# The second turn of the node stage of layers 0 and 1: from TensorE to VectorE squares and a move inside SBUF

## The reference, cut to what matters

```python
x = _layernorm(x + relu(concat(x, max_diff) @ W + b))        # layer 0
# layer 1
x = swish(x @ lin_W.T + lin_b)
h1 = swish((agg1 @ rel1.T + b + x @ root1.T) @ lin1.T + b)   # agg: sums over edges, 0 for most nodes
h2 = swish((agg2 @ rel2.T + b + x @ root2.T) @ lin2.T + b)
h = concat(h1, h2) @ cat_W.T + cat_b + x
for i in range(3):
    h = swish(h @ lins_W[i].T + lins_b[i]) + h
```

## Time and profile before

| | us |
|---|---|
| three executions | 5523.48, 5533.62, 5541.32 |
| median | 5533.62 |
| profiled execution: span from the first to the last instruction | 5523.1 |

### The profile page before, as it was taken

One profiled execution on the slowest core, in us unless ns is written; L12 is line 12 of the kernel. 1 busy time (PEld: TensorE's weight loads), 2 busy tenths in 40 slices (PEclk: granted clock), 3 DMA queues, 4 the chain that ended last, 5 costly groups with the idle time before them and its releaser, 6 DMA issues. The chain is left out here.

```text
span 5523.1 us, 86293 instructions
## 1 busy us (share of the span) xinstructions
PE 4551.3 (82%) x20518; PEld 2819.0 (51%) x20518; DVE 4178.7 (76%) x8262; ACT 3700.6 (67%) x9029; POOL 4058.2 (73%) x4123
## 2 busy tenths in 40 slices
PE   7999999999999999999999999999677756661000
PEld 4566666666666644444444477777455534451000
DVE  5766666666666658888888899999788854457776
ACT  4777777777777754444444488888688864446665
POOL 6777777777777768777777477777777767777777
PEclk9999999999999999999999999999855555665555
DMA  4556656556565646555555599999799867775443
GB/s 121 142 140 135 136 139 139 139 139 140 139 140 135 140 112 195 178 179 179 176 180 176 170 356 367 365 367 365 270 291 287 276 208 228 230 236 163 134 137 103
DMA packets 558505, 1084.50 MB, mean 196 GB/s; under 512 B 131183, under 2 KB 225065, under 8 KB 558279
## 3 DMA queue, kind: packets, MB, share of 16 engines
q1 hardware_dynamic: 452918, 931.29, 54.7%
q0 software_dynamic: 100352, 149.23, 11.2%
q10 hardware_dynamic: 5008, 1.60, 0.1%
HBM read 648.47 MB, written 438.76 MB: 197 GB/s over the span
## 5 line engine op out<-in xcount | busy, mean ns | idle before, releaser
L832 ACT ACTIVATE p_s<-p_ps,cols 128x512 f32<-128x512 f32 x588 | 404.5, 688 | 317.3 <-PE p_ps L774 207.7
L685 POOL DMA_INDIRECT p_xs<-in_x,src_cols x388 | 376.4, 970 | 221.1 <-DVE p_r L900 131.5
L1163 POOL DMA_INDIRECT ring_rows<-t_rows,home_cols x384 | 446.8, 1164 | 120.4 <-issue 88.6
L692 POOL DMA_INDIRECT home<-edge_row_cols,scatter_cols x392 | 414.8, 1058 | 131.2 <-issue 119.2
L182 POOL DMA_INDIRECT out<-u_res,scatter_cols x392 | 407.2, 1039 | 121.8 <-issue 117.8
L175 POOL DMA_INDIRECT u_rows<-t_rows,home_cols x392 | 388.6, 991 | 145.6 <-issue 118.5
L175 POOL DMA_INDIRECT ring_rows<-t_rows,home_cols x400 | 396.7, 992 | 128.2 <-issue 115.2
L685 POOL DMA_INDIRECT p_xd<-in_x,dst_cols x388 | 391.4, 1009 | 107.5 <-issue 89.0
L1172 POOL DMA_INDIRECT home_cols<-home,src_cols x376 | 379.8, 1010 | 111.4 <-issue 85.9
L1259 ACT ACTIVATE q_s<-q_ps,cols 128x512 f32<-128x512 f32 x294 | 202.1, 687 | 355.9 <-PE q_ps L1236 310.7
L900 DVE TENSOR_TENSOR p_r<-p_s,p_r 128x512 f32<-128x512 f32 x392 | 267.9, 683 | 194.0 <-ACT p_s L832 192.5
(11 more groups left out here) (310 smaller groups left out, 14446.8 us busy)
## 6 DMA issues: line engine op xcount, KB each, us to landing
p_x<-in_x SPq DMA_DIRECT2D x98, 512.0 KB, 6.5
t_rows<-p_o SPq DMA_DIRECT2D x98, 512.0 KB
hT<-ring_own SPq DMA_DIRECT2D x98, 512.0 KB
q_hn<-hT SPq DMA_DIRECT2D x98, 512.0 KB
r_h<-hT SPq DMA_DIRECT2D x98, 512.0 KB
r_x<-t_rows SPq DMA_DIRECT2D x98, 512.0 KB
t_rows<-r_y SPq DMA_DIRECT2D x98, 512.0 KB
t_rows<-r_x SPq DMA_DIRECT2D x98, 512.0 KB
```

Of the source, the lines that this page charges most:

```text
L685: nc.gpsimd.indirect_dma_start(out=rows[:, j, :], out_offset=None, in_=a["x"], in_offset=bass.IndirectOffsetOnAxis(ap=idx[:, j:j + 1], axi ...
L692: nc.gpsimd.indirect_dma_start(out=tab["home"], out_offset=bass.IndirectOffsetOnAxis(ap=s["scat"][:, k:k + 1], axis=0), in_=s["at"][:, k:k ...
L832: nc.scalar.activation(act_out[i][:, :], flat(bank_r), ACT.Silu, bias=col(LS0 + i)).then_inc(r_act[i], 1)
L1163: nc.gpsimd.indirect_dma_start(out=rows[:, e % 4, j, :], out_offset=None, in_=tab["t1"], in_offset=bass.IndirectOffsetOnAxis(ap=s["home"][ ...
```

## The change

The normalised rows `o` are no longer turned by TensorE. VectorE turns them in 32x32 squares into `o_turned` (`turn_squares`), at the head of a step, one step after ScalarE scaled them. When both blocks of a pair are turned, SyncE issues 16 transfers (`swap_groups`), each from 32 partitions of `o_turned` to 32 partitions of `x1T`, 256 numbers of 4 bytes in each partition, which bring every square to its place. The product by `lin` reads `x1T` in the order that `by_column` gives, and waits for these transfers.

The product by `lin` and the swish behind it move from lag 3 to lag 6, `R1` to `cat` from lag 4 to 7, the three rounds of `lins` from 5 to 8, the store of `hT` by one round. POOL's hold moves with them (`2 * e - 8`). The turn of `o` on TensorE, ScalarE's copy of it and the waits for both are gone. The pipeline has 206 steps (`NB + 10`), before 202, of which the last with work for TensorE is 203, before 200.

```diff
+def swap_groups(sp, across, turned, sem):
+    for a in range(4):
+        for c in range(4):
+            sp.dma_start(across[32 * c:32 * (c + 1), a], turned[32 * a:32 * (a + 1), c]).then_inc(sem, DMA)
+
+def by_column(across):
+    return across.rearrange("p a (j i) -> p j a i", j=G)
...
-        xT, x1T, xx = sb("p_xT", [P, 2, BLK]), sb("p_x1T", [P, 2, BLK]), sb("p_xx", [P, 4, BLK])
+        xT, xx = sb("p_xT", [P, 2, BLK]), sb("p_xx", [P, 4, BLK])
+        o_turned, x1T = sb("p_oT", [P, 2, 4, 2, P]), sb("p_x1T", [P, 2, 4, 2, P])
...
-        STEPS = 2 * QB + 4
+        STEPS = NB + 10
...  (SyncE)
-                n = t - 10
+                n = t - 12
                 if live(n, NB):
                     sp.wait_ge(r_added[2], n + 2)
                     sp.dma_start(tab["hT"][n // 2]...
+                n = t - 6
+                if live(n, NB):
+                    q = n // 2
+                    sp.wait_ge(o_squared, n + 2)
+                    after(sp, lined, n - 2)
+                    swap_groups(sp, x1T[:, q % 2], o_turned[:, q % 2], x1_in[q % 2])
...  (POOL)
-                    after(pool, r_added[0], 2 * e - 5)
+                    after(pool, r_added[0], 2 * e - 8)
...  (TensorE; lags 4 and 5 become 7 and 8)
-                n = t.back(3)
-                if n.live(NB):
-                    pe.wait_ge(applied, n.b + 1)
-                    ...
-                    transpose4(nc, bank_t, o[:, n.of(4)], s["ident"]).then_inc(x1_turned, 1)
...
-                n = t.back(3)
+                n = t.back(6)
                 if n.live(NB):
-                    pe.wait_ge(x1_copied, n.b + 1)
+                    q = n.pair()
+                    pe.wait_ge(x1_in[q.of(2)], landed(2, q, 16))
                     after(pe, h1_ready, n.b)
-                    nc.tensor.matmul(flat(bank_l), s["lin"][:, :], x1T[:, n.of(2), :],
+                    nc.tensor.matmul(flat(bank_l), s["lin"][:, :], by_column(x1T[:, q.of(2), :, n.slot % 2]),
                                      start=True, stop=True).then_inc(lined, 1)
...  (ScalarE)
-                n = t.back(3)
-                if n.live(NB):
-                    act.wait_ge(x1_turned, n.b + 1)
-                    after(act, lined, n.b - 1)
-                    nc.scalar.activation(x1T[:, n.of(2), :], flat(bank_t), ACT.Copy).then_inc(x1_copied, 1)
...  (VectorE, between residual(2) of lag 9 and residual(0) of lag 8)
+                n = t.back(3)
+                if n.live(NB):
+                    q = n.pair()
+                    dve.wait_ge(applied, n.b + 1)
+                    if n.past(4):
+                        dve.wait_ge(x1_in[q.of(2)], landed(2, q.back(2), 16))
+                    turn_squares(nc, o_turned[:, q.of(2), :, n.slot % 2].rearrange("p c (j i) -> p c j i", j=G),
+                                 o[:, n.of(4)]).then_inc(o_squared, 1)
```

More of the change, by code:

```diff
@@ L583, in nodes01 @@
         squares_saved, e_squared = [sem(f"squares_saved{i}") for i in range(2)], sem("e_squared")
-        (x_turned, x_copied, x1_turned, x1_copied, product, biased, summed, counted, guarded, rooted, scaled,
+        o_squared, x1_in = sem("o_squared"), [sem(f"x1_in{i}") for i in range(2)]
+        (x_turned, x_copied, product, biased, summed, counted, guarded, rooted, scaled,
          applied, lined, active, u_done1, u_done2, h1_ready, h2_ready, cat_done, r0_ready) = (sem(m) for m in (
-             "x_turned", "x_copied", "x1_turned", "x1_copied", "product", "biased", "summed", "counted",
+             "x_turned", "x_copied", "product", "biased", "summed", "counted",
              "guarded", "rooted", "scaled", "applied", "lined", "active", "u_done1", "u_done2", "h1_ready", "h2_ready",
@@ L737, in bank_t_left @@
                     pe.wait_ge(xd_copied, e.b + 1)
-                elif t.back(4).live(NB):
-                    pe.wait_ge(x1_copied, t.back(4).b + 1)
                 elif t.back(1).live(NB):
@@ L749, in step @@
                     transpose4(nc, bank_t, x[:, t.of(4)], s["ident"]).then_inc(x_turned, 1)
-                n = t.back(5)
+                n = t.back(8)
                 if n.live(NB):
@@ L755, in step @@
                                      start=True, stop=True).then_inc(r_done[0], 1)
-                n = t.back(4)
+                n = t.back(7)
                 if n.live(NB):
@@ L806, in step @@
                     pe.wait_ge(xd_in[e.of(2)], landed(2, e, G))
-                    if t.back(3).live(NB):
-                        pe.wait_ge(x1_copied, t.back(3).b + 1)
-                    elif t.live(NB):
-                        pe.wait_ge(x_copied, t.b + 1)
-                    else:
-                        bank_t_left(t)
+                    after(pe, x_copied, t.b + 1, NB)
                     transpose4(nc, bank_t, xd[:, e.of(2)], s["ident"]).then_inc(xd_turned, 1)
-                n = t.back(5)
+                n = t.back(8)
                 if n.live(NB):
```

12 lines of the change are left out of this document (4 added, 8 removed).

## The result

The changed kernel takes 5500.6 us in the median of six runs (5490.3 to 5509.0), the kernel before 5529.5 in six, the three of the table above among them (5520.9 to 5541.3). The ratio is 0.9949, with a 95% interval of 0.9936 to 0.9963: 29 us faster (20 to 35 by the interval), where 41 had been forecast. The profiled span is 5496.3 us against 5523.1, the mean granted clock 0.859 against 0.862.

A forecast was written before the change was run, and what follows sets the result against it. TensorE was taken to bound nodes01. Steady pairs -66, fill and drain +18, SyncE's pile-ups +7 gave -41 us, so 5533.6 became 5492.6 us; the range meant to hold 8 times in 10 was 5466 to 5524.

The forecast's parts named there:

- The bound and the steady pair: Steady steps of nodes01: TensorE sets the pace, VectorE's chain some even steps; a pair falls 0.70 to 19.24, 66 us off.
- The new turn hidden, strides free: VectorE's turn of the normed rows: 0.71 us, hidden in idle time; the product by lin reads squares at no cost.
- The transfers: SyncE's sixteen moves a round: stores 3.0, issues 7.6, landing 3.1, so 13.7 us after the scan; 5.4 to spare.
- the bound from the other side: Pessimistic figure for the moves: 0.68 us an issue, 10.9 in all, landing 6.5, together 20.4 us, too late.
- L: Time from the scan's end in an even step to the last landing of that round's moves; forecast 13.7 us.
- the third rival: Moves come late in every round, L823 waits for them; decides from 19.1 us after the scan; 5559 us, chance 0.10.
- The rules of the ports: Skill pages: 32-partition moves at half rate, some 2.4 us a round; a VectorE-GpSimd port lock could cost POOL 1.4 a pair.
- POOL as bound: Rival in nodes01: slower POOL transfers make the pair some 19.55 us; 5522 us, chance 0.13.
- TensorE as the bound throughout: Rival in nodes01: VectorE's chain gives way by 0.2 us, even step 9.08, pair 19.08; 5475 us, chance 0.17.
- Fill and drain, and the pile-ups: Start and end of nodes01: three more steps cost 18 us (14 to 22), SyncE's two pile-ups 7 (2 to 15).
- The stages behind `nodes01` are the same instructions.: Stages after nodes01: unchanged, so the sum gave them no term and the difference was put on the whole time.
- The end on the slower side: Chance of a slower kernel, over 5550 us: 0.09, with moves late in every round as the mechanism.

## Why the prediction came out as it did

**Sign and range right, and the changed stage gave 37.5 to 41.1 us of the 41 summed. The medians moved by 29, and where the other 12 went is only shown in part.** By the prediction's own steps:

- *The bound and the steady pair.* Right. TensorE lost its 0.43, and every second even step became VectorE's. Forecast were 9.09 and 9.29 for the two kinds of even step; measured 9.08 and 9.26, with 0.24 of wait. The sum put 0.05 for starting again into the even step and 10.00 for the odd one. Measured, the start costs 0.06 to 0.10 and stands in the odd step, which takes 10.06 to 10.08 from L772 to L772. The pair comes out at 19.24 as summed, instead of 19.94, so 0.70 x 95 = 66 us. That the even step is set by this chain is shown by moving 0.7 us out of it.
- *The new turn hidden, strides free.* Right: 0.70 us each. The passes of L829 stay at 0.59.
- *The transfers.* The conclusion was right, its number wrong. The term "16 issues 7.6 us" was taken from the nearest row in shape, L149, which reads DRAM (still 7.61 here). A move inside SBUF costs 0.68 to issue, the bound from the other side. The last issue ends 14.2 us after the scan, and the landing fits into the remaining 4.4. So in this round L lies between 14.2 and 18.6, not at 13.7, and under the 19.1 from which the third rival decides. The margin is smaller than the forecast said. The third rival had the right issue time and the wrong landing: it added 6.5 from a row that lies behind a queue of half-megabyte transfers.
- *The rules of the ports.* By the Trainium skill (SBUF — State Buffer, "Door 1: The DMA port swizzle") a move of 32 neighbouring partitions reaches half of the ports. No run here can show it, since the issues alone take 10.9 us for the 0.5 MB. By the Trainium skill (SBUF — State Buffer, "SBUF: two separate sides") VectorE and GpSimd lock a shared port for a whole instruction in some modes. In this trace the rows beside the new turns are mixed:

```profile
1214.12 1.52 POOL L712 DMA_INDIRECT home<-edge_row_cols,scatter_cols  x1 [0.30 <-issue]
...
1224.96 2.30 POOL L737 TENSOR_TENSOR p_rs<-p_guard,minus_half 128x12 f32<-128x12 f32 x1 [0.23 <-DVE p_guard L986]
...
1233.86 1.11 POOL L712 DMA_INDIRECT home<-edge_row_cols,scatter_cols  x1 [0.30 <-issue]
```

  The turns ran at 1214.67, 1225.93 and 1234.02. Beside the first a transfer took 1.52, beside the third 1.11. The power (L737) takes 2.30 or 2.67 from pair to pair, and so it did in the kernel before, where no such turn runs beside it:

```profile
1198.95 2.69 POOL L717 TENSOR_TENSOR p_rs<-p_guard,minus_half 128x12 f32<-128x12 f32 x1 [0.82 <-DVE p_guard L977]
...
1218.86 2.30 POOL L717 TENSOR_TENSOR p_rs<-p_guard,minus_half 128x12 f32<-128x12 f32 x1 [0.81 <-DVE p_guard L977]
```

  By the windows POOL is busy for 463 us in 31.2 pairs, 14.8 a pair, against 438 in 30.1, 14.6: two turns a pair added 0.3 us at most, not 1.4.
- *POOL as bound.* It didn't come, though the cause was seen in part (transfers of 1.33 and 1.52 in every second pair). POOL still waited 26.1 us for VectorE ahead of L705 and 6.9 ahead of L737 in 600 us, some 1.1 a pair. In the best version pairs of 19.07 went by, so it isn't the bound there either.
- *TensorE as the bound throughout.* It was a rival at 5475, held off by 0.2 us of VectorE. Moving one instruction on VectorE made it true.
- *Fill and drain, and the pile-ups.* 18 and 7 were forecast, 25 together. The starts of the turn of `x` and of `edges1` part them, in us:

| | before, first execution | before, second | changed |
|---|---|---|---|
| turn of `x`, step 6 | 80.8 | 77.9 | 75.0 |
| turn of `x`, step 195 | 1965.2 | 1962.2 | 1906.3 |
| start of `edges1` | 2024.3 | 2020.7 | 1983.2 |

  Up to step 6 the changed kernel is 5.8 or 2.9 us earlier, and behind step 195 it takes 17.8 or 18.4 more: fill and drain cost 12.0 or 15.5. Between the two steps it is 53 us shorter where the pairs give 66, so one-off waits cost 13, not 7. The sum of the stage came out at 41 because the one term was too high and the other too low, and against the second execution it is 37.5. That much of the agreement is luck. The largest of the one-off waits is the stall of step 20 (5.64), as forecast. The late move near the end was forecast too; it stands behind the sixteen loads of L149:

```profile
1942.53 1.12 PE L829 MATMUL p_ps<-p_x1T,lin 128*128 128x512 f32 x2 [1.17 <-DMA p_x1T<-p_oT]
```

  Two more weren't in the sum. The first product waited 1.79 us for its move at 80 us. And in four early steps VectorE, which does one-off work there (bias rows and the like), came late by 0.27 to 1.34 for the weight load of L792:

```profile
106.79 0.28 DVE L248 TENSOR_TENSOR bias_rest<-bias_rest,bias_part 3x128 f32<-3x128 f32 x1
...
111.08 1.12 PE L792 MATMUL p_ps<-p_r,lins 128*128 128x512 f32 x2 [0.89 <-DVE p_r L901]
```

  In the kernel before the same weight load waited once in these steps, for 0.32.
- *"The stages behind `nodes01` are the same instructions."* They are, and still the time of one of them isn't fixed: `edges3` took 504.7 and 516.6 us in two executions of the kernel before. This is a term that the sum put at nothing without a row: an allowance of some 14 us either way should have stood in the range. In the first pair of profiles it accounts for the 14.3 us between the stage's 41.1 and the span's 26.8 (519.6 - 504.7 = 14.9). It doesn't explain by itself why the medians of six executions lie 29 apart, for the kernel before has the long stage too; that stays open, as said above. In absolute terms 5492.6 was forecast and 5500.6 measured, 8 off and not 12, because the median of the kernel before came down from 5533.6 to 5529.5 with three more executions.
- *The end on the slower side.* The forecast gave "slower" one mechanism, a late move in each pair. Under the other conditions the changed kernel is slower by 2.5% with another mechanism, which isn't understood. It was beyond the trace of before, in which no such wait stands.

The best version shown is the changed kernel with the edge block's turn behind L971 and the small transfers spread: 5484.5 us in one execution beside 5530.9, but a ratio of 1.0314 in a slower group. Which of the two conditions a user has to expect isn't settled.

## What to carry to other kernels

Take out of the bound engine what another can do, then walk along the next engine's chain in each kind of step. Here 0.2 us of VectorE in every second even step cost 0.17 a pair, 16 us over the stage, and putting an instruction that isn't urgent behind the one that TensorE waits for gave it back. A queue that issues many small transfers is a resource like an engine: add up its issues by rows of the same direction (in this case 0.68 us for one from SBUF to SBUF, 0.47 from DRAM to SBUF), and look for the rounds in which one-off work stands in the same row. Before a difference of some tens of microseconds is laid on a change, look at the stages that it doesn't touch, in more than one execution.

## What was not expected of the hardware

- Sixteen moves of 32 partitions inside SBUF take SyncE 10.1 to 12.9 us to issue, 0.63 to 0.80 each; sixteen loads of 32 partitions from DRAM took 7.6. Whether the direction makes the difference or what stands in the queue wasn't tried.
- TensorE's slot behind a wait for VectorE was 0.96 us where it is 0.86 without one, so the wait cost more than its own length.
- The last stage took 504.7 and 516.6 us in two executions of one program, with gathers of 991 and 1021 ns in the mean.
- The same program, on the same kind of chip, took 5530 us or 6250. In the latter VectorE and ScalarE start up to several microseconds after the product that they wait for has ended (3.0 and 3.1 in the rows above). Moves that no steady step waits for at 5530 cost 4.4% there.
